# Attention in an audio-tower kernel: the upper causal quarters through two spare contraction rows a tile, and the softmax sums collected, inverted and spread by transfers

## What is computed

```python
h = tok(x)                                  # causal 32-tap filter over 375 tokens, then two 256x256 products
h = h + attn(layernorm(h))                  # 16 heads of 16, causal softmax, 376 rows
h = h + ffn(layernorm(h))                   # 2 shared experts, 16 routed with top 2

q = (x @ wq + bq).reshape(b, s, 16, 16).transpose(0, 2, 1, 3)      # k, v alike
scores = jnp.einsum('bhqd,bhkd->bhqk', q, k) / jnp.sqrt(16.)
scores = jnp.where(causal, scores, -jnp.inf)
weights = jax.nn.softmax(scores, axis=-1)
attn = jnp.einsum('bhqk,bhkd->bhqd', weights, v)
```

## Time and profile before

| | |
|---|---|
| three runs | 1859.0, 1865.74, 1866.49 us |
| the profiled execution, first to last instruction | 1852.8 us |
| TensorE busy, whole span | 1700.5 us (92%) |
| VectorE busy | 1437.1 us (78%) |
| ScalarE busy | 976.7 us (53%) |
| POOL busy | 1056.0 us (57%) |
| granted TensorE clock, mean | 0.959 |

### The profile page before, as it was taken

One profiled execution on the slowest core, in us unless ns is written; L12 is line 12 of the kernel. 1 busy time (PEld: TensorE's weight loads), 2 busy tenths in 40 slices (PEclk: granted clock), 3 DMA queues, 4 the chain that ended last, 5 costly groups with the idle time before them and its releaser, 6 DMA issues. The chain is left out here.

```text
span 1852.8 us, 49530 instructions
## 1 busy us (share of the span) xinstructions
PE 1700.5 (92%) x14718; PEld 1360.0 (73%) x14719; DVE 1437.1 (78%) x3985; ACT 976.7 (53%) x2048; POOL 1056.0 (57%) x1446
## 2 busy tenths in 40 slices
PE   5899999999999999999999998589999986988883
PEld 4677777777777777777777775368888876877773
DVE  4589899999999899899999996378888971455554
ACT  1166666666676666666666765333444422544441
POOL 4045555555555655655555556446777770567666
PEclk8899999999999999999999999679999997999996
DMA  2555556556556555555565453223333356999996
GB/s 76 80 132 152 141 128 158 142 119 166 141 135 144 147 147 138 135 154 142 123 162 141 123 147 99 109 74 105 126 120 120 122 155 169 286 327 326 323 331 220
DMA packets 226548, 291.13 MB, mean 157 GB/s; under 512 B 57142, under 2 KB 188954, under 8 KB 226458
## 3 DMA queue, kind: packets, MB, share of 16 engines
q1 hardware_dynamic: 190042, 186.14, 40.3%
q0 software_dynamic: 18048, 49.31, 8.2%
q10 hardware_dynamic: 18368, 54.64, 7.7%
HBM read 83.25 MB, written 129.69 MB: 115 GB/s over the span
## 5 line engine op out<-in xcount | busy, mean ns | idle before, releaser
L752 ACT ACTIVATE probs<-bank 128x376 f32<-128x376 f32 (+2 forms) x896 | 440.7, 529 | 272.9 <-PE bank L621 261.0
L843 DVE TENSOR_REDUCE neg_max<-bank 120x1 f32<-120x376 f32 (+2 forms) x896 | 507.0, 587 | 53.7 <-PE bank L587 49.7
L587 PE MATMUL bank<-k_rows,q_rows 64*128 64x128 f32 (+2 forms) x1536 | 403.7, 345 | 3.1 <-ACT probs L752 2.4
L621 PE MATMUL bank<-q_rows,k_rows 64*120 64x120 f32 (+2 forms) x1536 | 369.9, 336 | 3.9 <-ACT probs L752 3.6
L982 POOL TENSOR_SCALAR_AFFINE_SELECT probs<-probs 128x512 f32<-128x512 f32 (+1 forms) x384 | 232.4, 631 | 209.5 <-ACT probs L752 209.3
L604 PE MATMUL bank<-causal,own_row 56*120 56x56 bf16 (+4 forms) x1792 | 300.9, 248 | 8.7 <-DMA k_rows<-k_flat_hi 3.5
L587 PEld LDWEIGHTS bank<-k_rows,q_rows 64*128 64x128 f32 (+1 forms) x1536 | 246.2, 186 | 6.7 <-ACT probs L752 4.6
L2205 POOL DMA_INDIRECT y_got<-y_sorted,p_route x188 | 182.4, 970 | 119.7 <-issue 117.6
L621 PEld LDWEIGHTS bank<-q_rows,k_rows 64*128 64x128 f32 (+1 forms) x1536 | 229.8, 183 | 8.7 <-ACT probs L752 5.8
L604 PEld LDWEIGHTS bank<-causal,own_row 64*128 64x128 bf16 (+2 forms) x1792 | 153.4, 115 | 110.3 <-DVE neg_max L843 39.9
L1847 POOL DMA_INDIRECT x_sorted<-r_normed,route x188 | 184.3, 981 | 83.6 <-issue 59.0
(11 more groups left out here) (235 smaller groups left out, 4148.8 us busy)
## 6 DMA issues: line engine op xcount, KB each, us to landing
x_sorted<-zeros ACTq DMA_DIRECT2D x32, 816.0 KB, 3.8
y_sorted<-zeros ACTq DMA_DIRECT2D x32, 816.0 KB, 4.3
x_rows<-x_sorted SPq DMA_DIRECT2D x51, 512.0 KB, 6.4
y_sorted<-p_y_rows SPq DMA_DIRECT2D x51, 512.0 KB, 6.4
q_rows<-q_flat_hi SPq DMA_DIRECT2D x256, 94.0 KB
k_rows<-k_flat_hi SPq DMA_DIRECT2D x248, 94.0 KB
q_rows<-q_flat_lo SPq DMA_DIRECT2D x128, 94.0 KB
out_dram<-base SPq DMA_DIRECT2D x47, 256.0 KB, 5.0
```

Of the source, the lines that this page charges most:

```text
L587: last = eng.matmul(ps[0:T[t], m * w:(m + 1) * w], q[rows, slot, t * P:t * P + T[t]], k[rows, slot, 0:w], start=False, stop=(m == len(head ...
L621: last = eng.matmul(ps[0:T[t], m * w:(m + 1) * w], k[64 * c:64 * c + 64, slot, t * P:t * P + T[t]], q[64 * c:64 * c + 64, slot, t * P:S], ...
L752: eng.activation(probs[g % 2][0:T[t], first:first + len(heads), OFF[t]:OFF[t] + w], bank_exp[n % 2][0:T[t], 0:len(heads) * w].rearrange("k ...
L843: eng.tensor_reduce(dst, src, AX.X, ALU.max, negate=True).then_inc(max_taken, 1)
```

## The change

Two independent parts.

**Quarters.** `k_rows` gets -1e30 in rows 48 to 50 and 70 to 72 (one a tile) at the keys 64 and up of that tile, `q_rows` gets 1 there at the queries 0 to 63 of it. Their product hides the upper right quarter of each causal tile, in the maxima's scores and in Exp's. The second L604 product then needs only keys 0 to 63 of the tile, as its `dst` and `causal` slices say. The patterns are built by 2 memsets and 16 `affine_select`s on POOL in the first block, and `clear_rows` copies them in place of its memsets.

**Sums.** `keep` copies bank_pv once (64 rows a head pair as they are). SyncE gathers the 4 rows of sums of each of the two tiles into `sums[half]`, 64 partitions by 47 columns; VectorE inverts that in one instruction (at n = 10 for half 1, n = 23 for half 0); SyncE stores it to DRAM, waits, and loads it back with each row repeated over 16 partitions, for even and odd heads. POOL multiplies the even and the odd tile by it, adds them, and makes hi and lo as before. `join`, the shuffle, the four reciprocals and one of the two `keep` copies are gone.

The core of the diff:

```diff
@@ hide_later_keys
-                        dst = ps[0:d, 0:m * w].rearrange("q (m w) -> q m w", w=w)[:, :, t * P + first:t * P + d]
+                        dst = ps[0:d, 0:m * w].rearrange("q (m w) -> q m w", w=w)[:, :, t * P + first:t * P + first + part]
-                        eng.matmul(dst, own_row[group, h, 0:d], causal[group, h, 0:m, first:d],
+                        eng.matmul(dst, own_row[group, h, 0:d], causal[group, h, 0:m, first:first + part],
@@ keep (ScalarE)
-                        eng.wait_ge(joined, st.at(shift, 2, half))
+                        eng.wait_ge(attn_scaled, st.at(shift - 1, 2, half + 1))
-                    eng.activation(sum_of[e][:, :], bank_pv[:, 0:S], ACT.Copy, scale=strip_half[:, 1 - e:2 - e])
-                    eng.activation(attn_of[e][:, :], bank_pv[:, 0:S], ACT.Copy, scale=strip_half[:, e:e + 1])\
+                    eng.activation(heads_of[half][e][:, :], bank_pv[:, 0:S], ACT.Copy)\
@@ VectorE
-                HALF_1_AT = {10: (0, 1), 12: (2,), 14: (3,), 16: (4,)}
-                HALF_0_AT = {21: (0,), 23: (1, 2), 25: (3,), 26: (4,)}
+                HALF_1_AT, HALF_0_AT = 10, 23
+                def invert_sums(st, half, shift):
+                    eng.wait_ge(sums_gathered[half], st.at(shift, 32, 32))
+                    eng.reciprocal(inverse[half][:, :], sums[half][:, :]).then_inc(recip_done, 1)
@@ normalise (POOL)
-                    eng.tensor_tensor(attn_raw[:, :], attn_raw[:, :], recip[:, :], ALU.mult).then_inc(attn_scaled, 1)
+                    eng.wait_ge(recip_loaded, st.at(shift, 64, 32 * (half + 1)))
+                    eng.tensor_tensor(even[:, :], even[:, :], inverse_of[0][:, :], ALU.mult).then_inc(scaled_even, 1)
+                    eng.tensor_tensor(odd[:, :], odd[:, :], inverse_of[1][:, :], ALU.mult).then_inc(scaled_odd, 1)
...
+                    eng.tensor_tensor(attn_raw[:, :], even[:, :], odd[:, :], ALU.add).then_inc(attn_scaled, 1)
@@ SyncE
+                def gather_sums(st, half, shift):
+                    wait_alone(eng, even_kept, st.at(shift, 2, half + 1), passed_sp)
+                    wait_alone(eng, odd_kept, st.at(shift, 2, half + 1), passed_sp)
+                    for e in range(2):
+                        first = 16 * (1 - e)
+                        eng.dma_start(sums[half][32 * e:32 * e + 32, :], heads_of[half][e][first:first + 97:32, :])\
+                            .then_inc(sums_gathered[half], 16)
+                def spread_inverse(st, half, shift):
+                    wait_alone(eng, recip_done, st.at(shift, 2, half + 1), passed_sp)
...
+                    for e in range(2):
+                        eng.dma_start(bass.AP(inverse_dram.tensor, (16 * half + 9 * e) * S, [[2 * S, 4], [1, S]]),
+                                      inverse[half][32 * e:32 * e + 32, :]).then_inc(recip_stored[half], 16)
...
+                        wait_alone(eng, attn_scaled, st.at(shift, 2, half), passed_sp)
+                    wait_alone(eng, recip_stored[half], st.at(shift, 32, 32), passed_sp)
+                    for e in range(2):
+                        eng.dma_start(inverse_of[e][:, :], bass.AP(inverse_dram.tensor, (16 * half + 8 * e) * S,
+                                                                   [[S, 8], [0, 16], [1, S]])).then_inc(recip_loaded, 16)
@@ SyncE, step
                     if st.attend:
                         max_rows(st, 1, 0)
+                    if st.finish:
+                        gather_sums(st, 1, -1)
+                        spread_inverse(st, 1, -1)
...
                         rows(st, 0, "q")
...
                             rows(st, 0, "k")
+                    if st.attend:
+                        gather_sums(st, 0, 0)
                     if st.maxima:
                         max_rows(st, 0, 1)
+                    if st.attend:
+                        spread_inverse(st, 0, 0)
                     if st.finish:
                         store(st)
```

More of the change, by code:

```diff
@@ L37 @@
 MASKED = -3.0e38
+FAR = -1.0e30
 class Shapes:
@@ L195, in attention_phase @@
         odd_kept = sem("odd_kept")
-        joined = sem("joined")
-        sums_ready = sem("sums_ready")
+        scaled_even = sem("scaled_even")
+        scaled_odd = sem("scaled_odd")
+        inverse_cleared = sem("inverse_cleared")
+        sums_gathered = [sem(f"sums_gathered{h}") for h in range(2)]
         recip_done = sem("recip_done")
+        recip_stored = [sem(f"recip_stored{h}") for h in range(2)]
+        recip_loaded = sem("recip_loaded")
         attn_scaled = sem("attn_scaled")
@@ L312, in _, with fill_row @@
                     eng.memset(max_parts[h][:, :, :].bitcast(F32), 0.0)
+                def fill_row(at, first, last, value, signal):
+                    eng.affine_select(out=at[:, 0, first:last], in_=at[:, 0, first:last], compare_op=ALU.not_equal,
+                                      fill=value, base=-signal, pattern=[[0, last - first]], channel_multiplier=1)\
+                        .then_inc(rows_patterned, 1)
+                eng.memset(k_empty, 0.0).then_inc(rows_patterned, 1)
+                eng.memset(q_empty, 0.0).then_inc(rows_patterned, 1)
+                eng.wait_ge(rows_patterned, 2)
+                steps = 2
+                for c in range(2):
+                    for t in range(NT):
+                        far = t * P + P // 2
+                        fill_row(k_empty, far, t * P + T[t], FAR, FAR_ROWS[c] + t)
+                        fill_row(q_empty, t * P, far, 1.0, FAR_ROWS[c] + t)
+                        steps += 2
+                        eng.wait_ge(rows_patterned, steps)
+                for r in range(4):
+                    fill_row(k_empty, 0, S, 1.0, MAX_ROW + r)
+                    steps += 1
+                    eng.wait_ge(rows_patterned, steps)
             @block.tensor
@@ L904, in out_sum @@
                     last.then_inc(dense_read, 1)
-                def gather_sums(st, half, shift, piece):
-                    if piece == 0:
-                        wait_alone(eng, joined, st.at(shift, 2, half + 1), passed_dve)
-                        eng.stream_shuffle(sums[:, :], sums_swapped[:, :], [(i + 16) % 32 for i in range(32)])\
-                            .then_inc(sums_ready, 1)
-                    else:
-                        if piece == 1:
-                            eng.wait_ge(sums_ready, st.at(shift, 2, half + 1))
-                        cols = slice((piece - 1) * (S // 4), piece * (S // 4))
-                        eng.reciprocal(recip[:, cols], sums[:, cols]).then_inc(recip_done, 1)
+                def invert_sums(st, half, shift):
+                    eng.wait_ge(sums_gathered[half], st.at(shift, 32, 32))
+                    eng.reciprocal(inverse[half][:, :], sums[half][:, :]).then_inc(recip_done, 1)
                 def step(st):
@@ L942, in step @@
                             take_lo(st, f"nT{j}", nT[st.b % 2][1][:, j, :], nT[st.b % 2][0][:, j, :])
-                        if st.finish and n in HALF_1_AT:
-                            for piece in HALF_1_AT[n]:
-                                gather_sums(st, 1, -1, piece)
+                        if st.finish and n == HALF_1_AT:
+                            invert_sums(st, 1, -1)
                         if st.front and n in (13, 15):
@@ L951, in step @@
                                 take_lo(st, f"k{j}", k_flat[1][:, j, :], k_flat[0][:, j, :], bias=bias_k[:, j:j + 1])
-                        if st.attend and n in HALF_0_AT:
-                            for piece in HALF_0_AT[n]:
-                                gather_sums(st, 0, 0, piece)
+                        if st.attend and n == HALF_0_AT:
+                            invert_sums(st, 0, 0)
                         if st.mix and n == 27:
@@ L1013, in normalise @@
                     eng.tensor_tensor(lo, attn_raw[:, :], hi.bitcast(F32), ALU.subtract).then_inc(attn_done, 1)
-                def join(st, half, shift):
-                    if not (isinstance(st.i, int) and st.b + shift == 0 and half == 0):
-                        eng.wait_ge(sums_ready, st.at(shift, 2, half))
-                        eng.wait_ge(attn_done, st.at(shift, 2, half))
-                    eng.wait_ge(even_kept, st.at(shift, 2, half + 1))
-                    eng.wait_ge(odd_kept, st.at(shift, 2, half + 1))
-                    eng.tensor_tensor(attn_raw[:, :], attn_of[0][:, :], attn_of[1][:, :], ALU.add)
-                    eng.tensor_tensor(sums_swapped[:, :], sum_of[0][:, :], sum_of[1][:, :], ALU.add)\
-                        .then_inc(joined, 1)
                 def residual(st):
@@ L1053, in step @@
                                 mask(st, g, t)
-                        if g == 0 and st.finish:
-                            join(st, 1, -1)
                         if g == 1 and st.finish:
                             normalise(st, 1, -1)
-                        if g == 1 and st.attend:
-                            join(st, 0, 0)
                         if g == 3 and st.maxima:
```

34 lines of the change are left out of this document (24 added, 10 removed).

## The result

The changed kernel takes **2271.8 us** (median of 4 runs, 2265.5 to 2280.8) against 1865.9 before: a ratio of 1.218, 95% interval 1.215 to 1.221. It is slower, as forecast, but by 406 us where 180 were forecast, and outside the range of 1950 to 2130.

What follows compares the result with a forecast made beforehand. TensorE set the pace at 34.05 us a step; SyncE's queue would take over with a 39.9 us lap. 29 x 5.85 = 170 plus about 10 on 1852.8 gave 2033, plus 12.9 made 2046 us; range 1950 to 2130.

Steps and rivals of the forecast that it cites:

- Quarters, 0.4 us a step: TensorE's second L604 product: 0.10 us gained in each four-head unit, nothing in two-head and one-head units; 0.4 us a step.
- ScalarE, GpSimd, VectorE gain nothing by their lighter work: Fewer copies and reciprocals, some 6 us of VectorE work a step, give no time by themselves.
- The queue fills up and a lap through it sets the step: SyncE's queue: its 7.4 us idle a step is eaten up; a lap of 39.9 us replaces the 34.05 us step.
- steps 8 and 9: Gather of half 1 with its landing, 3.2 us; then VectorE's reciprocal, maxima of n = 11 and two signals, 1.0 us.
- Step 10: Last piece of the lap: TensorE begins n = 14, reusing that bank, and q is read out, 3.7 us.
- step 1: First piece of the lap: rows of half 0 on SyncE's queue, from q's release to the maxima's issue, 9.6 us.
- that wait ends before the queue next needs TensorE (for Exp's last unit), so it isn't added: TensorE's wait at n = 20 for `out`, behind the loads and five POOL instructions: 0 us added to the lap.
- Landings: Small transfers on SyncE's queue land 2.2 us from issue, allowed 1.5 to 4; two such landings lie on the lap.
- First rival: SyncE's queue keeps up: its idle 7.4 us hold the new issues, waits and landings; 1853 us, chance 0.06.
- Second rival: SyncE's queue fills up but half 1's gather lands in time for VectorE: 36.8 us a step, 1950 us, chance 0.15.
- The clock's rival: TensorE runs n = 14 and 15 with their q products at 1.2 GHz: 2.5 us more a step, 2118 us, chance 0.20.
- What would show it: Queue idle under 1 us for q, VectorE waiting about 2 for sums, TensorE waiting at n = 14 and n = 20.

Runs made afterwards that it cites:

- masks first: Changed kernel with the output projection at n = 25 and 26 and GpSimd's normalising of half 1 behind the third group's masks: 2134.9 us, lap 42.4.
- plain loads: Changed kernel with its four loads of inverses a step reading 128 plain DRAM rows in place of 8 rows 16 times each: 2157.1 us.
- spare transfers: Kernel before with the change's twelve transfers issued at the same places of SyncE's queue, from and to spare tiles, sums as before: 1969.5 us, lap 37.6.
- both edits: Changed kernel with the zero fills at n = 21 and 22 and half 0's reciprocal at n = 20: 2176.4 us, lap 43.6.
- masks first, fills later: Changed kernel with late output projection, half 1's normalising behind the third group's masks, and zero fills at n = 21 and 22: 2134.9 us.

## Why the prediction was right and wrong

- **Quarters, 0.4 us a step: right.** 0.105 a four-head unit (forecast 0.10), 0.44 a step, -12.9 us in all. All columns paid would have been 1.2 us a step. (The isolated-matmul formula of the Trainium skill, "TensorE: Matmul & The Clock Gate", Back-to-back issue gap, comes to that as an estimate; the measurement decides against it, and the page itself says that real streams depart from the formula.)
- **ScalarE, GpSimd, VectorE gain nothing by their lighter work: right.** VectorE is at 57% and the kernel slower.
- **The queue fills up and a lap through it sets the step: right in kind.** Rows of half 1 (8.7 for 8.6), store and x (2.6 for 2.6), maxima (3.1 for 2.85), inverses of half 0 (4.2 for 3.8) came as forecast; gather with landing and reciprocal took 2.9 for 4.2 in steps 8 and 9.
- **Step 10 failed, "TensorE begins n = 14 ... and q is read out", 3.7 us.** Neither in the changed kernel nor with masks first was that closing the one that counted. Behind the gather of half 1 the queue itself has half 1's stores, their landing and the loads before it reaches the rows of half 0, 4.9 us on average with masks first; one of them:

```profile
533.03 1.32 SPq L1147 DMA_DIRECT2D inverse_rows<-inverse  x2
...
538.03 2.52 SPq L1108 DMA_DIRECT2D q_rows<-q_flat_hi  x2
```

That is 1.2 us over step 10. The rows of half 0, slower to issue (9.0 us for twelve, 8.9 in the changed kernel, where 7.2 is their cost without fills in flight), take 10.8 for the 9.6 of step 1, another 1.2. These two are most of what the queue's ring of 42.4 has over 39.9.

- **The sentence that failed most: "that wait ends before the queue next needs TensorE (for Exp's last unit), so it isn't added".** It costs 4.7 us a step, the difference between the changed kernel and masks first. The queue needs something from behind n = 20 four times, the first at n = 23 (half 0's reciprocal), then out1, conv1 and the last Exp. The prediction followed one chain, took it for closed, and judged the second by its size and not by who waits behind it.
- **Landings "2.2, allowed 1.5 to 4".** The small ones are 1.7 to 1.8. The loads of half 1's inverses, which the sum left out as off the lap, are 9.1: the source of 8 rows (2.9 us of it, by the plain loads) and the zero fills (3.8), both overlooked; the fills' 816 KB transfers stood in the list of transfers of the page, and the DRAM side's 8 stood in the diff.
- **First rival** ("decides at 7.4 us added"): false, even for less: six transfers in half 0 (4.2 us with what lies between them) already cost 2.5 to 2.8 a step, six in half 1 alone nothing.
- **Second rival** (1950, chain doesn't close): its sum, 36.8 a step, is close to the 37.6 of the spare transfers, whose landings hold up nothing; there two landings aren't waited for, though, and the rows of half 0 cost more, so the closeness is in part luck. And the chain does close.
- **The clock's rival**: right in kind, about 2 us a step for a forecast 2.5, with the stall at n = 20 and not at n = 14 as its place.
- **What would show it**: the queue idling under 1 us for q held; the wait at n = 20 held, at three times its size; the one at n = 14 is 0.3 to 2.0 us and not in every step, where 2 to 4 were forecast, and VectorE's wait for sums near n = 10 was about 1.7 us, under the 2 forecast.

## What to carry to other kernels

Before a round trip is put into a queue, list every later wait of that queue and ask of each whether what it waits for stands, on its own in-order engine, behind something that waits for the round trip: one such pair makes a ring, and removing one link only shows the next. Read slack of a queue by place, not as a sum of idle time: the same six transfers were free behind one half's rows and some 2.7 us a step behind the other's, and the free six cost 1 us once the others were there. And split a change into its parts: here one of the two was a small gain that the other buried.

## What the runs showed of the hardware that was not expected

- A load of 128 partitions from 8 rows, each read 16 times, landed in 3.8 us and took 0.62 to issue; from 128 rows with the same bytes 2.5 and 0.33 to 0.44.
- Two fills of 816 KB on another engine's queue lengthened the landing of two 188 KB loads from 5.4 to 9.1 us, and the issues of the twelve row transfers behind them from 7.2 to 8.9 us. Moved, they did the same to their new company: 3.8 to 6.9 us for a landing (both edits), 1.2 to 3.2 us for two issues (masks first, fills later).
- Six transfers of 5.9 to 188 KB cost nothing by their bytes where the queue had room (half 1's alone, ratio 1.001).
